# Quantised attention: who copies the turned weights to integer levels, and how the first sequence's levels are shifted

## What is computed

```
def _fq(x, delta, zp, n_bits):
    xi = _round_ste(x / delta) + zp
    xq = jnp.clip(xi, 0.0, 2.0 ** n_bits - 1.0)
    return (xq - zp) * delta
...
    sim = jnp.einsum('bhid,bhjd->bhij', _fq(q, dq, 128.0, 8), _fq(k, dk, 128.0, 8)) * SCALE
    attn = jax.nn.softmax(sim, axis=-1)
    out = jnp.einsum('bhij,bhjd->bhid', _fq(attn, dw, 0.0, 8), _fq(v, dv, 128.0, 8))
```

## Time and profile before

| what | value |
|---|---|
| median of 3 runs | 2010.21 us (2009.72 to 2011.73) |
| the profiled execution's own time | 2007.97 us |
| its span, first to last instruction | 2006.2 us |
| TensorE busy | 1808.6 us, 90% of the span |
| VectorE, ScalarE, GpSimd busy | 1237.6, 1074.7, 905.3 us |
| mean granted TensorE clock | 0.933 of full speed |
| chain that ended last, by engine | TensorE 61%, VectorE 17%, ScalarE 10% |

### The profile page before, as it was taken

One profiled execution on the slowest core, in us unless ns is written; L12 is line 12 of the kernel. 1 busy time (PEld: TensorE's weight loads), 2 busy tenths in 40 slices (PEclk: granted clock), 3 DMA queues, 4 the chain that ended last, 5 costly groups with the idle time before them and its releaser, 6 DMA issues.

```text
span 2006.2 us, 34807 instructions
## 1 busy us (share of the span) xinstructions
PE 1808.6 (90%) x12481; PEld 1344.1 (67%) x12481; DVE 1237.6 (62%) x2220; ACT 1074.7 (54%) x3142; POOL 905.3 (45%) x1209
## 2 busy tenths in 40 slices
PE   4998988789799889889999999999999999999997
PEld 4887876466566656657667677676676676766766
DVE  5899995744654464463575665865746647365471
ACT  2232225665575475565575564655645656565662
POOL 4466554654463363363254443644444333333340
PEclk8999998788878878879999999999999999999999
DMA  7200000002000000000002000000000000000000
GB/s 226 92 11 6 11 6 6 1 7 90 1 6 6 1 6 6 0 6 7 1 7 90 1 7 6 7 7 1 7 6 2 12 1 7 22 7 1 12 1 11
DMA packets 31073, 35.66 MB, mean 18 GB/s; under 512 B 3164, under 2 KB 29752, under 8 KB 30520
## 3 DMA queue, kind: packets, MB, share of 16 engines
q1 hardware_dynamic: 30904, 33.44, 5.2%
HBM read 31.34 MB, written 2.10 MB: 17 GB/s over the span
## 4 chain that ended last, share of the span: by engine, by line
PE 61%; DVE 17%; ACT 10%; issue 6%; POOL 2%; SPq 2%; DMA 1%; DVEq 0%; POOLq 0%; ACTq 0%
PE ps L594 33%; PE ps L806 6%; PE ps L744 6%; PE ps L816 5%; PE ps L850 4%; ACT work L983 3%; ACT work L990 3%; DVE work L1183 3%; DVE xn L1037 2%; PE ps L607 2%; DVE rowmax L1187 2%; PE ps L831 2%; ACT hT L899 1%; PE ps L766 1%; POOL work L1376 1%
## 5 line engine op out<-in xcount | busy, mean ns | idle before, releaser
L594 PE MATMUL ps<-hT,w_slot 128*128 128x256 f32 x1696 | 410.1, 396 | 17.1 <-ACT hT L899 16.1
L1300 POOL TENSOR_TENSOR work<-KT,own_head 128x512 f32<-128x512 f32 x256 | 262.4, 1046 | 285.4 <-PE ps L806 179.9
L594 PEld LDWEIGHTS ps<-hT,w_slot 128*128 128x128 f32 x1696 | 323.5, 196 | 77.2 <-ACT hT L899 21.7
L990 ACT ACTIVATE work<-work,rowmax 128x128 f32<-128x128 f32 x768 | 244.9, 391 | 167.8 <-DVE rowmax L1187 167.0
L816 PEld LDWEIGHTS ps<-ident,work 128*128 128x128 f32 x1536 | 200.1, 153 | 170.0 <-issue 90.4
L983 ACT ACTIVATE work<-ps,rowmax,score_scale 128x128 f32<-128x128 f32 x512 | 229.3, 484 | 118.7 <-DVE rowmax L1191 118.3
L816 PE MATMUL ps<-ident,work 128*128 128x128 f32 x1536 | 266.4, 302 | 17.9 <-ACT work L990 17.0
L806 PE MATMUL ps<-work,QT 128*128 128x512 f32 x512 | 266.4, 605 | 10.0 <-POOL work L1300 4.9
L1376 POOL TENSOR_SCALAR work<-work,winv 128x128 f32<-128x128 f32 x512 | 185.0, 382 | 167.7 <-DVE winv L1203 165.3
L1217 DVE RECIPROCAL O<-ps 128x128 f32<-128x128 f32 x128 | 122.3, 955 | 174.6 <-PE ps L850 173.9
L976 ACT ACTIVATE work<-ps 128x512 f32<-128x512 f32 x256 | 150.7, 596 | 91.4 <-PE ps L816 91.2
(11 more groups left out here) (131 smaller groups left out, 3170.3 us busy)
## 6 DMA issues: line engine op xcount, KB each, us to landing
ctx_in<-in_ctx SPq DMA_DIRECT2D x32, 256.0 KB, 2.7
w_slot<-in_L_xattn_W SPq DMA_DIRECT2D x2, 1024.0 KB, 6.2
w_slot<-in_L_xattn_ff_w SPq DMA_DIRECT2D x1, 2048.0 KB, 11.5
w_slot<-in_L_xattn_ffn_w SPq DMA_DIRECT2D x2, 1024.0 KB, 9.8
w_slot<-in_L_xattn_w SPq DMA_DIRECT2D x2, 1024.0 KB, 10.0
out<-x_all SPq DMA_DIRECT2D x8, 256.0 KB, 2.1
x_all<-in_x SPq DMA_DIRECT2D x1, 1536.0 KB, 11.4
pad<-in_mask_Bx1x1xS_fk SPq DMA_DIRECT2D x1, 1024.0 KB, 7.6
```

What stands on the lines that cost most here:

```text
L594: mm = pe.matmul(dst, lhsT(k), rhs(k), start=(k == 0 and not onto), stop=(k == chunks - 1 and not more))
L990: ex = act.activation(prob[i % NPF][:, tok(h)], src[:, tok(h)], ACT.Exp, bias=shifts[:, at:at + 1])
L1300: pool.tensor_tensor(KB[u % NK].rearrange("p (h k) -> p h k", h=HU), keys, own_head[:, e:HC:2].unsqueeze(2).broadcast_to([P, HU, S]), ALU. ...
```

## The change

For the first sequence of each phase (units 0 to 3) the copy of the turned weights moves from ScalarE to VectorE, in a new function `levels`, called at step i for unit i - 4, behind `shift` and `inverses` and ahead of `quant_outputs`. It takes the minimum with MAGIC + 255 and subtracts MAGIC, so it gives the level itself; no constant product is needed, and `values` for j = 0 leaves out its four matmuls with `below`. The sign of `out_scale` then differs between the sequences, so it has a column for each. The second sequence stays as it was; ScalarE waits once, at unit 4, for all four VectorE copies, and VectorE once, at unit 0, for the copies of the phase before.

```
-        out_scale = sb("out_scale", [P, 2])
+        out_scale = sb("out_scale", [P, 2 * G])
...
-                    for n in range(4):
+                    for n in range(2 if j == 0 else 0, 4):
...
-                                           start=(n == 0), stop=(n == 3))
+                                           start=(n == (2 if j == 0 else 0)), stop=(n == 3))
...
-                    if 0 <= u < U:
+                    if (UJ if quant else 0) <= u < U:
...
                         if quant:
-
+                            if u == UJ:
+
+                                act.wait_ge(s["PT_ready"], U * ap + UJ)
                             act.activation(PTb[u % 2], bank(2 + u % 2), ACT.Relu, bias=top[:, 0:1], scale=-1.0).then_inc(s["PT_ready"], 1)
...
+                def levels(u):
+
+                    if u == 0:
+
+                        dve.wait_ge(s["PT_ready"], U * ap)
+                    dve.wait_ge(s["o_ps"], U * ap + u + 1 - 2)
+                    dve.wait_ge(s["PT_ps"], U * ap + u + 1)
+                    dve.tensor_scalar(PTb[u % 2], bank(2 + u % 2), MAGIC + 255.0, MAGIC, ALU.min, ALU.subtract).then_inc(s["PT_ready"], 1)
+
                 def quant_outputs(j):
...
-                                      out_scale[:, arg["quant"]:arg["quant"] + 1], None, ALU.mult).then_inc(s["o_ready"], 1)
+                                      out_scale[:, G * arg["quant"] + j:G * arg["quant"] + j + 1], None, ALU.mult).then_inc(s["o_ready"], 1)
...
+                    if quant and 0 <= i - lag < UJ:
+                        levels(i - lag)
...
-                    dve.tensor_scalar(out_scale[:, n:n + 1], deltas[:, 4 * n + 2:4 * n + 3], deltas[:, 4 * n + 3:4 * n + 4], -1.0,
-                                      ALU.mult, ALU.mult)
+                    for j in range(G):
+                        dve.tensor_scalar(out_scale[:, G * n + j:G * n + j + 1], deltas[:, 4 * n + 2:4 * n + 3], deltas[:, 4 * n + 3:4 * n + 4],
+                                          -1.0 if j else 1.0, ALU.mult, ALU.mult)
```

## The result

| | before | after |
|---|---|---|
| median | 2010.53 us (4 runs, 2009.72 to 2011.73) | 1997.95 us (4 runs, 1997.4 to 2000.41) |
| profiled execution, its span | 2007.97, 2006.2 us | 2000.41, 1998.7 us |
| mean granted clock | 0.933 | 0.929 |

The ratio after to before is 0.9939 [0.9927, 0.9951], which is 12 us of 2010. Timed again beside the experiments, the same kernel gave 0.9949 [0.9936, 0.9962], 10 us. The forecast was a gain of 8.2 us, a time of 2002.0 us in a range of 1994 to 2010; both measurements lie inside that range and show a larger gain than the sum. Ratios leave out one run of experiment 2, which took 2618.87 us at a granted clock of 0.639.

The account below looks back on a forecast made before the run. The prediction took TensorE to bound the quantised phases after a latency-bound start. Matmuls saved 0.51 us in each of 16 phases, 8.2 us, and moved copies counted nothing: 2010.2 - 8.2 = 2002.0 us, range 1994 to 2010.

Parts of the forecast that it names:

- Bound: Each quantised phase: a latency-bound start, then from the transposes of the scaled input a TensorE-bound stretch, where TensorE's savings count.
- TensorE's term: Values blocks of units 1 to 3 gain 0.19, 0.19 and 0.13 us, 0.51 a phase; unit 0's gain is hidden.
- The case's own range: From the bounds of 6.2 and 11.5 us and 0.3 us at f2: 1998 to 2005 us.
- ScalarE's copies: 64 copies of 0.69 us, 44 us in all, leave ScalarE ahead of later exponentials; costed at nothing on the path.
- The cover at f2: Heavy phases: hid ready 0.3 us before f2; removing ScalarE copies keeps it ahead, no loss, perhaps 0.3 us gain.
- VectorE's copies: 64 copies arrive on VectorE at 0.75 us each, 48 us in all, beside the path.
- Unit 0's copy hidden: Between inverses and scale: scale starts 0.25 us late, but its stall behind GpSimd's spread swallows that; xn unchanged.
- 1 (the clock comes back sooner): Lower-clock stretches end sooner in four phases, 7 us more gain, 1995 us; chance 0.18.
- 2 (later): Lower-clock stretches end later in four phases, 7 us lost, 2009 us, no measurable change; chance 0.15.
- 3 (given back): Another engine sets f0's hid or the phase-end quantising; TensorE only waits longer, time stays 2010 us; chance 0.07.
- 4 (slower): Unit 0's copy pushes scale out of its cover, 1.0 us a phase, 8 us slower, 2018 us; chance 0.08.
- The signs I had named: Among them: L831 at 768 matmuls, its pieces near 0.35 and 0.20 us, VectorE copy 0.69 to 0.75, f2 without gap.

Follow-up runs that it names:

- experiment 2: Kernel before with only the first sequence's copies moved to VectorE (255 minus the level), all constant products kept: 2004.39 us, 0.9974.
- the delays: Three or eight tiny VectorE operations ahead of each quantised phase's first shift: kernel before 2011.91 and 2015.05 us, kernel after 2001.31 and 2003.83 us.
- Experiment 6: Kernel after without the second sequence's constant products either: 1998.93 us with copies split between VectorE and ScalarE, 2000.72 us with all copies on ScalarE.
- experiment 1: Kernel before with only the first sequence's constant products left out, copies staying on ScalarE as a Relu: 2003.37 us, 0.9967.
- Experiment 5: Kernel after with two more VectorE copies of unit 0 into spare tiles ahead of the real one: 2007.91 us, 0.9992.
- experiment 8: Kernel before with each ScalarE copy of units 0 to 3 made twice, once into a spare tile: 2036.48 us, 1.0127.
- split form: Kernel after without any constant products, copies on VectorE for the first sequence and ScalarE for the second: 1998.93 us, 0.9954.

## Why the prediction was right, and where its working was off

The time came out inside the range, but not by the sum alone: the sum had all of the gain in TensorE's matmuls, the runs have a good half of it there and the rest in a term that the sum put at nothing. That the total still lies near the forecast is in part luck, since the first term was too large while the second was missing.

**Bound.** Right for the heavy phase's dense stretch, and what TensorE saves behind a start comes off (rest 5.0 us, with the delays 4.4 and 5.1). Experiment 6 shows where that ends. A light phase isn't without a gap: its last block waits 0.51 us for ScalarE's copy of unit 7, before and after alike.

**TensorE's term, 8.2 us in 16 phases, 7.1 in the 14 measured.** Right in kind, somewhat too large. The whole change took 6.3 us off the time behind the starts (rest 5.0, clock loss 1.3), but that has the moved copies in it. The products alone took off 4.4 us there with the copies on ScalarE (before to experiment 1, 394.0 to 389.5) and 4.5 with them on VectorE (experiment 2 to after, 392.2 to 387.7), where two traces of the kernel before differ by 2.4; the rest of experiment 1's 6.6 us lies in the starts (1.9 in 14 phases). The price of a block was read rightly, since the chain's pieces agree (0.54 to 0.33 and 0.33 to 0.22, 0.21 and 0.11 us); in experiment 1, 1.3 us of it went into more wait ahead of f2. The case's own range was added up loosely: 2010.2 less 11.5 and less 0.3 in 8 phases is 1996.3 and not 1998, and 2010.2 less 6.2 is 2004.

**ScalarE's copies, "I cost this at nothing".** This is the step that failed: the term measured 5.2 us. The cover at f2 was argued rightly: with the products gone and the copies kept, f2 waited; with both, hid is ready 1.0 us ahead of f2 (591.07 + 0.48 against 592.56 us). But "nothing on the path asks for them sooner" was too strong. Moving the copies alone gained 5.2 us with an interval of 3.2 to 7.2, and doubling them lost 25.6. The groups of waits of the kernel before gave no sign of it. TensorE's L831 and its weight loads do wait for copies there, 4.0 and 6.8 us, but these waits belong to the last two units of the light phases, whose copies the change leaves on ScalarE, and they stand in the kernel after as they were:

```profile
PEld ps L831 <- ACT work L976: 6.8, 16, 0.7
...
PE ps L831 <- ACT work L976: 4.1, 8, 0.5
```

With no wait for the copies of units 0 to 3 in the kernel before and one in every phase with each copy doubled, ScalarE stood within 1.7 us of TensorE's path (three more copies of 0.57 us come ahead of unit 2's block); that tells what more work for it costs, not what less brings.

Where the 5.2 us sit is only partly known. In the phases of experiment 2 the rest fell by 0.7 us, the starts by 1.1 and the clock loss by 1.1, against the mean of before, 2.9 in all, about what two traces of one kernel differ by. The granted clock of the runs says a little more: the eight runs of experiment 2 all have 0.933 or 0.934 and a mean of 2004.5 us; of the 20 runs of before beside them, seven have 0.933 to 0.935 and a mean of 2007.8, the other thirteen 0.928 to 0.932 and 2010.5. So some 3 us of the gain hold against runs at a like clock, and the remainder is that the kernel before is often at a lower one.

The starts can be read further. A quiet start takes 9.86 us; the longer ones, 10.1 to 11.2 in the first trace of before, follow heavy phases and run while the other stream's out-projection is at the lower clock. The timelines and windows (columns as above) of one such start, of the kernel before:

```profile
675.95 3.31 PE L594 MATMUL ps<-w_slot,OT 128*128 128x256 f32 x8
...
679.36 0.69 DVE L1059 TENSOR_TENSOR x_all<-ps,x_all 128x512 f32<-128x512 f32 x1 [2.06 <-PE ps L594]
...
680.95 0.46 ACT L983 ACTIVATE work<-ps,rowmax,score_scale 128x128 f32<-128x128 f32 x1 [0.84 <-DVE rowmax L1191]
...
676.50:679.50 3.00, 3.00 (x8) 1.78 (x6) 0.91 (x3) 3.00 (x14) 0.00 (x0) 0.50 0.00 0
```

of the same kernel in its second trace:

```profile
678.60 1.99 PE L594 MATMUL ps<-w_slot,OT 128*128 128x256 f32 x8
...
676.50:679.50 3.00, 1.60 (x6) 1.01 (x7) 2.82 (x7) 0.37 (x2) 0.91 (x1) 1.00 0.02 5
```

and of the kernel after:

```profile
676.67 0.69 DVE L1061 TENSOR_TENSOR x_all<-ps,x_all 128x512 f32<-128x512 f32 x1 [1.50 <-PE ps L594]
...
678.26 0.46 ACT L985 ACTIVATE work<-ps,rowmax,score_scale 128x128 f32<-128x128 f32 x1 [0.25 <-DVE rowmax L1193]
```

The same eight matmuls take 3.31 us in one trace, with the clock at 0.50 for most of it, and 1.99 in the other with the clock at 1.00. When they are slow, the residual sum on VectorE comes late, and with it the next exponential (0.84 us idle on ScalarE for 0.25). The two go together closely: over both traces of before, out-projections of 2.72, 2.85, 2.90, 3.07, 3.31 and 3.45 us at this place go with starts of 9.96, 10.09, 10.14, 10.31, 10.53 and 10.67 us, a microsecond for a microsecond. In the kernel after the block took 2.63 to 2.75 us in the same four phases (4, 8, 9, 12) of both traces, which costs a start 0.1 us at most; in the first trace of before it took 2.90 to 3.78 in six. So nearly all of the 3.5 us that the starts gave is the lower clock meeting this block for less of its time. Why either half of the change makes it so wasn't found, and stays open.

**VectorE's copies, 0.75 us.** They took 0.683 us (675 to 692 ns), below the row I had taken and below my lower bound of 0.69. The row of 0.745 us has a column operand and fp32 output; which of the two makes the difference no run shows. The Trainium skill (VectorE: DVE Perf Modes, TRN2 errata) gives an estimate of 0.66 us for such a copy, closer than my row. The price didn't matter much: VectorE is busy for 10.66 of the 23.10 us of the heavy phase's dense stretch.

**Unit 0's copy hidden.** Right in the result (9.86 and 9.88 us to the transposes), with another cover than I named. Scale didn't start late at all, 8.38 and 8.39 us behind the first exponential: before, VectorE stood idle for 0.54 us until GpSimd's rstd was there, and the copy went into that gap, ending 0.2 us behind rstd. The stall behind spread, which I had counted on, stayed as it was (1.34 us for both scale operations). Experiment 5 shows that second cover at work, and how thin it is: of 1.28 us more it took half.

**Rivals.** 1 (the clock comes back sooner): in part. Much of the gain beyond the matmuls lies in the starts, where the lower clock met the out-projection for less time, and the medians lie between the forecast and its 1995. 2 (later): not in the change; the time behind the starts at clock 0.50 fell (clock loss 55.1 to 53.7). The rule that I named beside this rival (the Trainium skill, TensorE: Matmul & The Clock Gate, HAM oscillation: the gate falls after idle time) agrees in direction with experiment 8, where TensorE was idle for 15.6 us more and the time behind the starts at clock 0.50 grew by about 21 us; that the gaps, 0.3 to 1.0 us each, brought it wasn't shown. 3 (given back): refuted for the change, L804 and f2 didn't grow; in experiment 6 it is what happened. 4 (slower): refuted, though experiment 5 reaches its arithmetic: two more copies cost 9 us.

**The signs I had named.** The right ones came but one: 768 matmuls, 0.33 and 0.22 us in the chain, xn in its place, no gap at f2; the VectorE copy, 0.683 us, fell just under its 0.69 to 0.75. The phases moved closer by 0.7 us on average (9.8 over 14) where 0.51 was forecast. The last sign, the total at clock 0.50, seems to have come out wrong: 210 us in the earlier trace rows, 225 in the kernel after, more than the 10 us that I had allowed.

```profile
521.50:534.50 13.00, 10.94 (x42) 0.50 0.00 0
...
sum 225.00, PE 197.61; mean PE 12.35
```

But the 210 was a miscount. The kernel before has three more short stretches at 0.50, two of them

```profile
676.50:679.80 3.30, 3.30 (x8) 0.50 0.00 0
837.00:840.30 3.30, 3.28 (x8) 0.50 0.00 0
...
sum 9.90, PE 9.88; mean PE 3.29
```

which my 16 windows left out, so the total rose from 220 to 225 us, inside the 10. They are also the ones that fall on the out-projections at phase starts. That the total rose at all while the clock loss behind the starts fell says that more of it lies within the starts, where it costs only what reaches into that block or past the transposes.

## What to carry to other kernels

An engine that the bottleneck hardly waits for can still stand a microsecond or two behind it. A term put at nothing for that reason needs a bound: here taking 64 copies from ScalarE brought 5.2 us and adding 64 cost 25.6, so neither can be read from the other. Before taking a group of waits as the sign of a cost, see which units and phases it belongs to (the 4.0 and 6.8 us on the copies belonged to the other sequence). And when time is split into clock loss and the rest, read the idle time beside it, since a wait at the lower clock stands in both.

Where matmuls overlap on column strips, price those that go by the offset between them (0.13 and 0.19 us a block), not by their busy time (0.24). And a delay goes first into whatever gap is already there: list all the gaps around the place (here 0.54 us on rstd, then the stall behind spread) before deciding that an operation is hidden.

## What the runs showed that was not expected

Doubled ScalarE copies took 34 us of ScalarE's time and cost 25.6 us; over 14 phases, 15.6 us of the loss were TensorE's idle time behind the starts, 3.8 its longer busy time there and 1.5 the starts.

Less TensorE work didn't always give time: 256 further matmuls left out were worth nothing measurable (0.9954 for 0.9949, 0.9965 for 0.9967), while the first 256 gave 6.6 us. In the split form 3.6 us less busy time met 3.2 us more idle time.

A delay ahead of each phase cost 2.8 us of 4.3 added, and 4.4 of 9.1, as the starts became shorter than in the plain kernel (140.4 and 139.0 for 142.0 us over 14 phases). The delay holds back the first exponential but not the out-projection, which starts 0.71 and 1.01 us ahead of it after heavy phases in place of 0.53; so a slow out-projection lengthens the start less.
